# Attention: the eight PSUM banks dealt anew, four for scores and two for maximum products in place of three and three

## The chip, the cores and the metric

The kernel runs on one core of one Trainium2 chip. The metric is the device time of one execution in microseconds (us). A core has a matrix engine (TensorE, PE in the profile; its weight loads are shown apart as PEld), VectorE (DVE), ScalarE (ACT), GpSimd (POOL) and the engine that issues most of the DMAs (SyncE, SP). Matmul results go to PSUM, which has eight banks of 512 fp32 values in each of 128 partitions. Each engine works through its own instructions in order, and semaphores tie the engines together.

## The reference

One transformer layer on 2 x 2048 tokens of width 512, in fp32: attention with low-rank keys and values, and then a mixture of experts. Only the core of the attention bears on this case:

```python
scores = jnp.einsum('bhqd,bhkd->bhqk', q, k) / jnp.sqrt(jnp.float32(DH))     # b=2, h=16, q=k=2048, DH=32
scores = jnp.where(causal[None, None], scores, -jnp.inf)
attn = jax.nn.softmax(scores, axis=-1)
out = jnp.einsum('bhqk,bhkd->bhqd', attn, v)
```

The softmax subtracts the maximum of each row of scores. So the kernel needs that maximum before it takes the exponentials.

## The kernel before, in words

The program has four stages one after the other: the projections, the attention (`phase_attention`), the output projection with the shared expert, and the routed experts. The change is in the second one alone.

**Units and steps.** The 16 heads are taken four at a time and the two batches apart, which makes 8 groups. The 2048 queries of a group are cut into four chunks of 512. A unit is one group and one chunk q, so there are 32 units. A unit goes through its key tiles of 128 keys in the order that `ORDER[q]` lists (4, 8, 12 or 16 tiles). For each tile there are two steps, one for heads 0 and 1 and one for heads 2 and 3. That gives 640 steps. The four tiles of a unit that lie on the diagonal are masked: 128 of the 320 tiles, 256 of the 640 steps.

**What a step does.** TensorE computes two score products, one for each head: `b_st`, L1008, 128 keys by up to 512 queries. In a masked step VectorE then adds the mask to both banks (`b_st<-b_st,b_sooner`). ScalarE takes the exponential of each bank and writes it to one half of a buffer `b_pt` in SBUF (L928). Later TensorE uses the exponentials of both steps of a tile. The four value products (`values`, `b_ob`, L1021, 8 rows in the trace) come in the second step of the next tile. For a part of the tiles there are also four products with a matrix of ones (`count_ones`, `b_sb`, L1035), which sum the exponentials. For the other tiles (`POOL_TILES`) GpSimd adds the exponentials up in `b_acc` (L749), and one group of matmuls at the unit's end (`finish`, L1043) sums that. The values, ones and finish groups are called heavy groups below.

**The maximum products.** Between these, the same matrix engine computes the scores of a later unit a first time, transposed, only to get their row maxima: `b_mx`, L985, 128 queries by up to 512 keys. VectorE reduces each such bank to one column (L868, or on the diagonal L865, which adds the mask as it reduces). There are 1280 of them. Once a unit's maxima are complete, its row of negative maxima is made by four transposes into a `b_mx` bank (L992), ScalarE copies it (L934), and a DMA puts it under the queries as one more row. All 1312 of these (maxima and turns) form one list, `stream`. `attention_plan` decides how many of them each step takes, and `item_shares` puts a step's share in three places: after the first score product, after the heavy group, and after the second score product.

**What sets the order.** Every engine's instructions are written out by the loops in the order of the steps. The banks tie them together. A score product with the running number 2n+j goes to bank (2n+j) % NST and waits until the exponential NST before it is done (L1001). Item i of the list goes to bank i % NMX and waits until VectorE has reduced item i-NMX (or until ScalarE has copied it, where that was a turn). The values of a tile wait for the tile's last exponential, which is the one four before the second score product of their step (`values`). The scores hold NST banks, the maximum products NMX, `b_ob` and `b_sb` one each: eight in all.

**The mask.** The two banks of a masked step are one instruction (L890) where they lie next to each other, and two instructions (L894) where one is the last and one the first bank of the ring (`mask`).

Of the kernel before, what the change touches and what calls it, by code (L numbers as in the profile page):

```python
# [601 lines left out]
def phase_attention(nc, x, w, scratch, ahead, keep, heads):  # L602
# [7 lines left out]
    units, steps, first_step = attention_steps()  # L610
    stream, start, upto, turn_at, turn_step = attention_plan(units, steps, first_step)
    NS, NU = len(steps), len(units)
    NPB, NST, NMX = 8, 3, 3
    KR = HG * DH - DH
    MROW = KR

# [1378 lines left out]
def program(nc, ins, out):  # L1995
# [15 lines left out]
    with ExitStack() as ctx:  # L2011
        al = Alloc(nc, ctx)
        ahead = Ahead(al)
        keep = {
            "ident": al.sb("ident", [P, P]),
            "expert": al.sb("expert", [P, NB], I32),
            "place": al.sb("place", [P, NB], I32),
            "entry": al.sb("entry", [P, NB, TPB, 3], U32),
            "x": [tile[:].rearrange("p k n -> p (k n)").rearrange("p (t n) -> p t n", t=TPB) for tile in (ahead.oin, ahead.rin)],
            "x_in": [al.sem(f"e_rows_in{n}") for n in range(2)],  # L2020
            "entries_in": [al.sem(f"e_first_entries_in{n}") for n in range(2)],
            "weights_in": [al.sem(f"e_weights_in{n}") for n in range(2)],
        }
        with ExitStack() as early:
            heads = Heads(Alloc(nc, early))
            phase_project(nc, x, w, scratch, ahead, keep, heads)
            phase_attention(nc, x, w, scratch, ahead, keep, heads)
        begun = First(al, ahead)
        phase_shared(nc, x, w, scratch, ahead, keep, begun)
        phase_experts(nc, keep, w, scratch, begun, out)  # L2030
# [23 lines left out]
```

## Time and profile before

| | |
|---|---|
| time, median of 3 runs | 2332.29 us (2331.23 to 2332.98) |
| the profiled execution | 2336.36 us, of which the span shown is 2334.6 us |
| attention stage in the span | from about 233 to about 1440 us |
| PE busy over the span | 2192.8 us (94%) |
| DVE, ACT, POOL busy | 1480.2, 1027.3, 1165.0 us (63, 44, 50%) |

The profile gives busy and idle times of each engine. The end of a matmul is modelled: one product of 512 columns is shown with 0.40 us, while the next one can start 0.23 us behind it. So a stop of TensorE is longer than the idle time shown for it, by up to 0.17 us. The idle time shown before a weight load (PEld) is mostly time in which TensorE was still at work on a heavy group.

### The profile page before, as it was taken

To read this page: it belongs to the slowest core of one execution; us is meant where nothing else is said; L and a number is where in the kernel's file an instruction comes from. 1 tells how busy PE (TensorE), PEld (TensorE's weight loads), DVE (VectorE), ACT (ScalarE), POOL (GpSimd) and SP (SyncE) were. 2 spreads that over 40 slices of the span, in tenths; PEclk is the share of its full clock that TensorE was granted. 3 is DMA by queue.
4 is the path that set the end of the run, shared out by engine and by line. 5 is a ranking of instruction groups with operands and counts; after the bars stand their busy time and mean duration, and the time that the engine had idled before them with its cause. 6 is when DMAs were issued, how large, how long until landed. Compare 5 with 4: busy or idle time off the path is not lost. (4 is left out here: it accounts for less than half of the span.)

```text
span 2334.6 us, 32228 instructions
## 1 busy us (share of the span) xinstructions
PE 2192.8 (94%) x11695; PEld 1377.6 (59%) x11695; DVE 1480.2 (63%) x3296; ACT 1027.3 (44%) x1925; POOL 1165.0 (50%) x730
## 2 busy tenths in 40 slices
PE   6999999999999999999999997899997999999999
PEld 5777544444444444444444432677775788888887
DVE  4665886767766676676776742667565455556554
ACT  3333255555655555555555555131222343434433
POOL 1010166556665565655666557364644445544544
PEclk9999699999999999999999988899998999999999
DMA  5678702313123141151412111434433756666662
GB/s 167 246 256 268 171 24 51 77 37 91 37 55 74 38 91 37 46 142 38 91 37 55 53 30 44 127 121 134 137 105 119 240 184 222 197 215 208 207 212 87
DMA packets 168254, 278.66 MB, mean 119 GB/s; under 512 B 28571, under 2 KB 71067, under 8 KB 168096
## 3 DMA queue, kind: packets, MB, share of 16 engines
q1 hardware_dynamic: 145152, 210.43, 31.0%
q0 software_dynamic: 22944, 66.19, 9.1%
q8 instruction: 92, 1.51, 0.3%
q14 instruction: 66, 0.54, 0.1%
HBM read 191.25 MB, written 88.71 MB: 120 GB/s over the span
## 5 line engine op out<-in xcount | busy, mean ns | idle before, releaser
L928 ACT ACTIVATE b_pt<-b_st 128x512 f32<-128x512 f32 (+3 forms) x1280 | 612.5, 535 | 478.6 <-DVE b_st L890 192.0
L749 POOL TENSOR_TENSOR b_acc<-b_acc,b_pt 128x1024 f32<-128x1024 f32 (+1 forms) x256 | 593.0, 2346 | 215.8 <-ACT b_pt L928 215.2
L868 DVE TENSOR_REDUCE b_mpart<-b_mx 128x1 f32<-128x512 f32 x768 | 512.2, 686 | 186.9 <-PE b_mx L985 184.5
L1008 PE MATMUL b_st<-b_q,b_k 97*128 97x512 f32 (+2 forms) x1280 | 499.1, 403 | 57.1 <-ACT b_pt L928 53.7
L985 PE MATMUL b_mx<-b_k,b_q 96*128 96x512 f32 (+2 forms) x1280 | 510.9, 414 | 6.7 <-DVE b_mpart L868 3.3
L985 PEld LDWEIGHTS b_mx<-b_k,b_q 96*128 96x128 f32 x1280 | 249.5, 196 | 264.3 <-DVE b_mpart L868 149.7
L1008 PEld LDWEIGHTS b_st<-b_q,b_k 97*128 97x128 f32 x1280 | 243.4, 192 | 264.9 <-ACT b_pt L928 239.7
L1021 PE MATMUL b_ob<-b_pt,b_v 128*32 128x512 f32 (+3 forms) x2560 | 305.5, 549 | 1.1 <-ACT b_pt L928 1.1
L865 DVE CUSTOM_DVE_ANT_0 b_unread<-b_mx,b_later 128x384 bf16<-128x384 f32 (+3 forms) x512 | 244.6, 484 | 91.0 <-PE b_mx L985 90.5
L749 POOL TENSOR_TENSOR b_acc<-b_pt 128x1024 f32<-128x1024 f32 x48 | 113.4, 2379 | 269.5 <-ACT b_pt L928 269.5
L1774 POOL DMA_INDIRECT e_rows<-out_dram,entry x78 | 92.8, 1190 | 128.9 <-DMA out_dram<-e_rows,entry 111.9
L1902 ACT ACTIVATE e_sg<-e_fb 128x512 f32<-128x512 f32 (+3 forms) x69 | 36.6, 530 | 253.3 <-PE e_fb L79 253.3
L1866 POOL DMA_INDIRECT out_dram<-e_rows,entry x78 | 78.2, 1002 | 107.2 <-DVE e_rows L1947 90.8
L1933 DVE TENSOR_TENSOR e_hf<-e_sg,e_fb 128x512 f32<-128x512 f32 (+3 forms) x69 | 41.6, 603 | 131.3 <-ACT e_sg L1902 131.3
L1035 PE MATMUL b_sb<-b_pt,b_ones 128*32 128x512 f32 (+3 forms) x1152 | 116.5, 477 | 0.0
L890 DVE TENSOR_TENSOR b_st<-b_st,b_sooner 128x256 f32<-128x256 f32 x171 | 73.1, 428 | 67.5 <-PE b_st L1008 67.3
L77 PE MATMUL e_fb<-e_xh,e_w_split 128*128 128x512 f32 (+3 forms) x288 | 104.4, 362 | 1.8 <-PEq L1269 1.8
L1021 PEld LDWEIGHTS b_ob<-b_pt,b_v 128*32 128x32 f32 x2560 | 50.7, 108 | 90.4 <-issue 47.0
L79 PE MATMUL e_fb<-e_xl,e_w_split 128*128 128x512 f32 (+3 forms) x288 | 103.3, 359 | 0.0
L78 PE MATMUL e_fb<-e_xh,e_w_split 128*128 128x512 f32 (+3 forms) x288 | 103.0, 358 | 0.0
L77 PE MATMUL e_fb<-e_xh,e_w_guh 128*128 128x512 f32 (+3 forms) x264 | 96.9, 367 | 0.0
L79 PE MATMUL e_fb<-e_xl,e_w_guh 128*128 128x512 f32 (+3 forms) x264 | 95.9, 363 | 0.0
(251 smaller groups left out, 3692.9 us busy)
## 6 DMA issues: line engine op xcount, KB each, us to landing
b_q<-scr_qh SPq DMA_DIRECT2D x64, 256.0 KB, 4.6
b_k<-scr_kh SPq DMA_DIRECT2D x64, 256.0 KB, 4.0
sw_raw<-in_L_ffn_w_gate_dram SPq DMA_DIRECT2D x12, 704.0 KB, 4.5
sw_raw<-in_L_ffn_w_up_dram SPq DMA_DIRECT2D x12, 704.0 KB, 6.9
a_xin<-in_L_attn_x_dram POOLq DMA_DIRECT2D x8, 1024.0 KB, 5.8
scr_qh<-wo SPq DMA_DIRECT2D x8, 1024.0 KB, 5.0
scr_ql<-oin SPq DMA_DIRECT2D x8, 1024.0 KB, 7.2
scr_kh<-sw_raw SPq DMA_DIRECT2D x8, 1024.0 KB, 4.3
```

The costliest lines, as they stand in the source:

```text
L77: nc.tensor.matmul(out, wh, xh, start=first, stop=False)
L78: nc.tensor.matmul(out, wl, xh, start=False, stop=False)
L79: return nc.tensor.matmul(out, wh, xl, start=False, stop=last)
L749: g.tensor_tensor(out[:, :, lo:], so_far[:, :, lo:], pt[n % NPB][:, :, lo:], ALU.add).then_inc(s_add, 1)
L865: v.tensor_tensor_reduce(unread[i % NMX][:, 0:w], mxb[i % NMX][:, 0:w], later[:, CH - w:], 1.0, -3e38, ALU.add, ALU.max, part).then_inc(s_ ...
L868: v.tensor_reduce(part, mxb[i % NMX][:, 0:w], AX.X, ALU.max).then_inc(s_red, 1)
L928: act.activation(pt[n % NPB][:, j, lo:], stb[:, (2 * n + j) % NST, lo:], ACT.Exp, scale=SCALE).then_inc(s_exp, 1)
L985: ins = pe.matmul(bank[:, 0:max(w, 2 * P)], qb[0:KR, h, q * CH + t * P:q * CH + (t + 1) * P], kb[0:KR, h, at:at + max(w, 2 * P)], start=Tr ...
L1008: pe.matmul(stb[:, (2 * n + j) % NST, lo:], kb[:, h, at:at + P], qb[:, h, q * CH + lo:(q + 1) * CH], start=True, stop=True).then_inc(s_st, 1)
L1021: ins = pe.matmul(ob[h * DH:(h + 1) * DH, lo:], vbuf[:, kt, h * DH:(h + 1) * DH], pt[(2 * m + h // 2) % NPB][:, h % 2, lo:], start=(kt == ...
L1035: ins = pe.matmul(sb[h * DH:(h + 1) * DH, lo:], ones[:], pt[(2 * m + h // 2) % NPB][:, h % 2, lo:], start=(kt == begin), stop=(kt == ORDER ...
L1774: g.indirect_dma_start(out=tile[:, t, :], in_=rows, out_offset=None, in_offset=at).then_inc(sem, 16)
```

## The change

Two numbers. The scores get four banks and the maximum products two:

```diff
-    NPB, NST, NMX = 8, 3, 3
+    NPB, NST, NMX = 8, 4, 2
```

The order of TensorE's instructions stays the same, and so do those of ScalarE, GpSimd and SyncE. What changes is the bank that each product goes to, and with it the instruction that it waits for. A score product now waits for the exponential four before it, and an item for the reduction two before it. The plan of the items does not look at either number.

TensorE, before, in a tile that GpSimd sums (step 275 and the two behind it; `b_mx` are maximum products, `b_st` scores; the heavy group of values stands just ahead and just behind):

```order
L985 MATMUL b_mx1<-b_k,b_q 128x512 [waits b_partial_max]
L1008 MATMUL b_st<-b_q,b_k 128x512 [waits b_exp_made]
L985 MATMUL b_mx2<-b_k,b_q 128x512 [waits b_partial_max]
L1008 MATMUL b_st<-b_q,b_k 128x384 [waits b_exp_made]
L985 MATMUL b_mx0<-b_k,b_q 128x512 [waits b_partial_max]
L1008 MATMUL b_st<-b_q,b_k 128x384 [waits b_exp_made]
L985 MATMUL b_mx1<-b_k,b_q 128x512 [waits b_partial_max]
L1008 MATMUL b_st<-b_q,b_k 128x384 [waits b_exp_made]
```

TensorE, changed, at the same place:

```order
L985 MATMUL b_mx1<-b_k,b_q 128x512 [waits b_partial_max]
L1008 MATMUL b_st<-b_q,b_k 128x512 [waits b_exp_made]
L985 MATMUL b_mx0<-b_k,b_q 128x512 [waits b_partial_max]
L1008 MATMUL b_st<-b_q,b_k 128x384 [waits b_exp_made]
L985 MATMUL b_mx1<-b_k,b_q 128x512 [waits b_partial_max]
L1008 MATMUL b_st<-b_q,b_k 128x384 [waits b_exp_made]
L985 MATMUL b_mx0<-b_k,b_q 128x512 [waits b_partial_max]
L1008 MATMUL b_st<-b_q,b_k 128x384 [waits b_exp_made]
```

The sequence is the same. The third maximum product now goes to the bank of the first and the fourth to that of the second. Before, only the fourth met a bank of this group again.

VectorE, before, in steps 276 and 277 (both masked; `b_mpart` are the maxima, `b_unread` is the output of L865 that nobody reads):

```order
L890 TENSOR_TENSOR b_st<-b_st,b_sooner 128x2x128 [waits b_scores_made]
L865 ISA b_unread1,b_mpart1<-b_mx1,b_later 128x512 [waits b_item_made]
L865 ISA b_mpart1 128x1
L868 TENSOR_REDUCE b_mpart1<-b_mx2 128x1 [waits b_item_made]
L894 TENSOR_TENSOR b_st<-b_st,b_sooner 128x128 [waits b_scores_made]
L894 TENSOR_TENSOR b_st<-b_st,b_sooner 128x128
```

VectorE, changed, at the same place:

```order
L890 TENSOR_TENSOR b_st<-b_st,b_sooner 128x2x128 [waits b_scores_made]
L865 ISA b_unread0,b_mpart1<-b_mx0,b_later 128x512 [waits b_item_made]
L865 ISA b_mpart1 128x1
L868 TENSOR_REDUCE b_mpart1<-b_mx1 128x1 [waits b_item_made]
L890 TENSOR_TENSOR b_st<-b_st,b_sooner 128x2x128 [waits b_scores_made]
```

With four banks the two banks of a step always lie next to each other, so the pairs of L894 become single instructions of L890 (85 steps). Nothing else moves on VectorE.

## Rows read from the trace of the kernel before

**Rows 1.** Busy time by stretch, attention stage: us, PE, PEld, DVE, ACT, POOL, clock, DMA, GB/s
```profile
233.00:1440.00 1207.00, 1137.36 (x6607) 527.86 (x6605) 826.03 (x2176) 659.18 (x1379) 714.20 (x310) 0.97 0.26 62
```
**Rows 2.** Costliest groups of the page: busy, mean ns, idle before, releaser
```profile
L868 DVE TENSOR_REDUCE b_mpart<-b_mx 128x1 f32<-128x512 f32 x768 | 512.2, 686 | 186.9 <-PE b_mx L985 184.5
L1008 PE MATMUL b_st<-b_q,b_k 97*128 97x512 f32 (+2 forms) x1280 | 499.1, 403 | 57.1 <-ACT b_pt L928 53.7
L985 PE MATMUL b_mx<-b_k,b_q 96*128 96x512 f32 (+2 forms) x1280 | 510.9, 414 | 6.7 <-DVE b_mpart L868 3.3
L890 DVE TENSOR_TENSOR b_st<-b_st,b_sooner 128x256 f32<-128x256 f32 x171 | 73.1, 428 | 67.5 <-PE b_st L1008 67.3
```
**Rows 3.** The tile b_st, who waited for it (us, times)
```profile
  PEld b_st L1008: 241.3, 375
  PE b_st L1008: 53.7, 107
```
**Rows 4.** Timeline 780.6 to 783 us: start, duration, instruction
```profile
780.62 0.50 PE L985 MATMUL b_mx<-b_k,b_q 96*128 96x512 f32 x1
781.15 1.89 DVE L868 TENSOR_REDUCE b_mpart<-b_mx 128x1 f32<-128x512 f32 x3 [0.58 <-PE b_mx L985]
781.19 0.40 PE L985 MATMUL b_mx<-b_k,b_q 96*128 96x512 f32 x1
781.60 0.40 PE L985 MATMUL b_mx<-b_k,b_q 96*128 96x512 f32 x1
782.01 0.40 PE L985 MATMUL b_mx<-b_k,b_q 96*128 96x512 f32 x1
782.51 1.06 PE L1021 MATMUL b_ob<-b_pt,b_v 128*32 128x512 f32 x8
```
**Rows 5.** Timeline 783 to 786.8 us, the masked step behind it
```profile
783.49 0.87 ACT L928 ACTIVATE b_pt<-b_st 128x384 f32<-128x384 f32 x2 [1.51 <-DVE b_st L890]
783.51 0.50 PE L985 MATMUL b_mx<-b_k,b_q 96*128 96x512 f32 x1
784.04 0.44 PE L1008 MATMUL b_st<-b_q,b_k 97*128 97x384 f32 x1
784.05 0.69 DVE L868 TENSOR_REDUCE b_mpart<-b_mx 128x1 f32<-128x512 f32 x1
784.32 0.40 PE L985 MATMUL b_mx<-b_k,b_q 96*128 96x512 f32 x1
784.55 0.40 PE L1008 MATMUL b_st<-b_q,b_k 97*128 97x512 f32 x1
784.65 0.49 DVE L894 TENSOR_TENSOR b_st<-b_st,b_sooner 128x128 f32<-128x128 f32 x2
785.26 1.85 ACT L928 ACTIVATE b_pt<-b_st 128x384 f32<-128x384 f32 x4 [0.89 <-DVE b_st L894]
785.80 0.50 PE L1008 MATMUL b_st<-b_q,b_k 97*128 97x512 f32 x1 [0.85 <-ACT b_pt L928]
786.38 0.40 PE L1008 MATMUL b_st<-b_q,b_k 97*128 97x512 f32 x1
786.71 0.53 PE L1021 MATMUL b_ob<-b_pt,b_v 128*32 128x384 f32 x4
```
**Rows 6.** Timeline 742 to 745.6 us, a group with six items
```profile
742.97 0.75 PE L985 MATMUL b_mx<-b_k,b_q 96*128 96x256 f32 x2
743.48 0.68 DVE L868 TENSOR_REDUCE b_mpart<-b_mx 128x1 f32<-128x512 f32 x1
744.33 0.50 PE L1008 MATMUL b_st<-b_q,b_k 97*128 97x512 f32 x1 [0.61 <-ACT b_pt L928]
745.48 0.64 PE L1021 MATMUL b_ob<-b_pt,b_v 128*32 128x512 f32 x4
```
**Rows 7.** Busy time by stretch, two neighbours (columns as in Rows 1)
```profile
700.00:719.00 19.00, 18.03 (x112) 8.51 (x108) 14.49 (x39) 10.28 (x24) 14.09 (x6) 1.00 0.36 76
719.00:726.00 7.00, 6.86 (x23) 2.28 (x23) 2.40 (x6) 2.53 (x6) 0.00 (x0) 0.52 1.10 236
```

## The prediction, written before the changed kernel had run

> **What bounds the kernel now.** I read the busy table first, then the stretches, the costliest groups, the waits by tile and last the timeline of a few steps. The change touches the attention stage alone. There TensorE is busy 1137 of 1207 us [rows 1]. VectorE with 826 us, ScalarE with 659 and GpSimd with 714 are well below. So TensorE sets the pace, and only its stops can give or take time: whatever the others gain or lose counts when TensorE waits for it. Its stops are shown before the scores, 53.7 us in 107 waits, all for an exponential [rows 2, 3]. Before the maximum products it stops for 3.3 us only [rows 2]. The reader is to see here that the bank kind that gets one more is the one that waits, and the kind that gives one up does not wait today. The question is how far below "one bank too few" the maximum products are.
>
> **Units of time.** In [rows 4, 5], at full clock, a product of 512 columns follows another at 0.23 us (784.32 to 784.55). The first product behind a heavy group costs 0.34 (780.62 to 781.19 is 0.57 for two). The first result of a group reaches VectorE after 0.53 (780.62 to 781.15). A reduction takes 0.69, but a second one starts 0.60 behind it: three in 1.89 are 2 x 0.60 + 0.69. The exponential of ScalarE that begins at 785.26 has 384 columns. The pair before it took 0.87 for two, so one takes 0.48 and ends at 785.74. TensorE goes on at 785.80, so a release costs 0.06.
>
> **Part A, one bank fewer for the maximum products.** A heavy group takes TensorE 1.0 us (782.51 to 783.51), long enough for VectorE to catch up. So what counts is how many items stand between two heavy groups. I counted that in the order of TensorE's instructions: none to two items in 298 gaps, three in 64, four in 55, five in 33, six in 27, and seven or eight in 8 (one more, at the stage's start, is left out). With alternating scores the items of a gap start at 0, 0.57, 1.03, 1.50, 1.96 and 2.43 us. With two banks item k waits for reduction k-2, that is until 0.53 + 0.60 (k-3) + 0.69 + 0.06: 1.28 for the third, 1.88, 2.48 and 3.08 for the fourth to sixth. With three banks these times hold one item later, so today the fifth goes at 1.96 and the sixth at 2.48. The loss per gap is 0.25, 0.38, 0.52, 0.60 and 0.60 us. The sum is 64 x 0.25 + 55 x 0.38 + 33 x 0.52 + 27 x 0.60 + 8 x 0.60 = 16 + 21 + 17 + 16 + 5 = 75 us.
>
> A gap of the trace bears this out. In [rows 4] the four items start at 780.62, 781.19, 781.60 and 782.01. Reductions one and two end at 781.84 and 782.44. With two banks the third goes at 781.90 and the fourth at 782.50, which is 0.49 late, and the values behind it start 0.49 late. Nothing hides that: the values are on TensorE itself.
>
> Some of it is hidden, though. In gaps of six TensorE stands for an exponential anyway. In [rows 6] the second of the two items at 742.97 goes at about 743.3, and with two banks it would wait for the reduction that ends at 744.16, so until 744.22. But the score behind it stands until 744.33 today. The loss at the group's end is about 0.1 in place of 0.60. I take 0.45 off for each of the 27 gaps of six: -12. **Part A is +63 us.** Its bounds are 0 (TensorE stops only 3.3 us for these banks now, and if the wait fell wholly into other waits nothing would be seen) and 93 (each reduction at 0.69 without the overlap, which makes the losses 0.29, 0.51 and 0.69).
>
> **Part B, one bank more for the scores.** The stops to be had are the idle time of 53.7 us. To it comes for each of the 107 the tail of the modelled end, 0.40 - 0.23 = 0.17, so 18 us. The 375 - 107 = 268 waits that only the weight load shows [rows 3] lie inside that tail, at about 0.09 each, so 24 us. Together that is 96 us. Not all of it comes back. The masked step in [rows 5] shows why. Its stops are 784.04 (0.19 late, since 783.51 + 0.34 is 783.85) and 785.80 (784.55 + 0.23 is 784.78, so 1.02 late). With four banks the first goes at 783.85. The next item goes at 784.1 and the score after it at 784.4. The one that stood until 785.80 now waits for an exponential that ended at 784.36 (783.49 + 0.87), so it goes at 784.6. But the score behind that needs the exponential that ends at 785.74. That one hangs on the mask at 784.65, which VectorE takes only once its reduction (784.05) is done. So it goes at 785.80, the values start at about 786.2 in place of 786.71, and 0.51 of 1.21 us is gained, 42%. The wait moves on by two products. I take 42% of 96: **part B is -40 us.** Bounds: 0 (the chain score, mask, exponential, values holds everything) and -96.
>
> **Small edits.** In 85 steps two mask instructions become one. [Rows 5] show the two with 0.49, and the single one takes 0.43 [rows 2]. That is 0.06 times 85 = 5 us on VectorE, of which a part is on the path: -0 to -5, I take -1. The turns lose their third bank too. An item two behind a turn then waits for ScalarE's copy, but a heavy group or a few products stand between, so I put 0 for 32 of them, and at most 32 x 0.3 = 10.
>
> **Sum.** +63 - 40 - 1 + 0 = +22 us. The profiled execution took 2336.4, so it would be 2358.5. The median of the runs lies 4.1 lower, so I forecast 2355.
>
> **A rule that speaks against the change.** In 719 to 726 us the granted clock is 0.52, so mostly the lower of its two levels (1.2 GHz), where it was 1.00 in the 19 us before [rows 7]. Ahead of it TensorE had stood a few times before scores. The Trainium skill says in "TensorE: Matmul & The Clock Gate", section "A second HAM failure mode: psum-queue depth-cycling", that a kernel that cycles through PSUM banks idles so often and so briefly between matmul groups that the clock gate swings between its levels. By that rule part A's many small stops would bring more such stretches, and part B's would take some away. The attention shows a mean clock of 0.97 [rows 1], which is 0.03 x 2 x 1207, about 70 us, at half speed at most, and costs 36 us at most. The rule has its own case below.
>
> **The rivals.**
> - **The fourth score bank is worth more** (16%). Masks and exponentials follow earlier scores, so the gain in one gap may help the next. For it: all of TensorE's shown waits stand before scores [rows 2]. Against: the wait in [rows 5] hangs on the mask. With 96 us back and +63 it is -33, so about 2300. It wins from the point where part B returns more than two thirds of its stops. The Trainium skill ("Perfetto Trace Analysis", section "Optimization Strategy") says that the same gap repeated on the engine that should be saturated can mean too little PSUM. By it alone the kind with the visible gap is the one to widen. The trace agrees on the gap, but not on who pays for it.
> - **It cancels out** (10%). The two examples show it, +0.49 in one gap and -0.51 in the next. If the gaps were equally many, about 2332. Against: the counts (187 gaps with three or more items, 128 masked tiles).
> - **The fourth bank gives nothing** (12%). The values wait for the exponential four before the second score of their step, which is just what that score waits for with four banks. If the values stand in its place, B is -5 and the sum +57: 2390.
> - **The clock** (10%). With more short stops the half-speed time grows by a half: 18 us more, 2373. The other way, it falls by as much, and 2337 results.
>
> The likeliest case, +22 with 2340 to 2370, gets 52%. A measurement of this kernel tells about 0.2%, 5 us, from no change. Faster than that: the first rival and half of the second, 0.20. Same: 0.07. Slower: 0.73. The range that holds 8 in 10 runs from 2314 to 2392, from half-way into the first rival to the third.
>
> **What would show it.** Right: the idle time before L1008 falls from 57 to under 30 us and the one before L985 rises from 7 to 35 or more, released by L868. The timeline has items that stand for a reduction in gaps of three and more, above all in tiles that GpSimd sums. L894 is gone. The stages outside 233 to 1440 us keep their times, and VectorE's busy time falls by about 5 us. Wrong: idle time before L985 that stays under 15 us, or idle time that moves to the values (L1021).

## The result, and the profile after

The changed kernel takes 2367.92 us (median; 2366.97 to 2370.01), and the one before 2332.64. The ratio is 1.0154 (95% interval 1.0136 to 1.0171), so the change costs 35 us. The profiled executions give 2366.97 and 2336.36 us, a difference of 30.6, and the spans differ by the same 30.6. The prediction said 2355, in a range of 2314 to 2392.

All of it lies in the attention. By stretch the changed kernel shows (us, then PE, PEld, DVE, ACT and POOL busy, granted clock, DMA share, GB/s):

```profile
233.00:1471.00 1238.00, 1170.17 (x6607) 520.76 (x6605) 831.20 (x2091) 658.35 (x1377) 714.26 (x310) 0.97 0.24 60
1471.00:2365.20 894.20, 846.66 (x4103) 680.56 (x4095) 522.25 (x883) 290.96 (x425) 427.77 (x388) 0.97 0.53 167
```

The same TensorE instructions (6607) now take 1238 us where [rows 1] have 1207. What follows takes 894.2 us, against 2334.6 - 1440 = 894.6 before. The costliest groups of the page have changed places:

```profile
L868 DVE TENSOR_REDUCE b_mpart<-b_mx 128x1 f32<-128x512 f32 x768 | 516.2, 687 | 220.7 <-PE b_mx L985 216.5
L985 PE MATMUL b_mx<-b_k,b_q 96*128 96x512 f32 (+2 forms) x1280 | 550.4, 436 | 48.4 <-DVE b_mpart L868 29.5
L1008 PE MATMUL b_st<-b_q,b_k 97*128 97x512 f32 (+2 forms) x1280 | 480.5, 392 | 10.4 <-ACT b_pt L928 9.3
L890 DVE TENSOR_TENSOR b_st<-b_st,b_sooner 128x256 f32<-128x256 f32 x256 | 109.2, 426 | 75.9 <-PE b_st L1008 75.9
```

The idle time before the scores fell from 57.1 to 10.4 us, and the one before the maximum products rose from 6.7 to 48.4 [rows 2]. Idle time alone gives only -5 for the two. The rest is shown as busy time, which rose by 33 us over the stage (1137 to 1170). A product of 512 columns that follows a stop, or a heavy group, is shown with 0.50 us in place of 0.40, and the mean of L985 rose from 414 to 436 ns.

The place of [rows 4] shows it in the changed kernel (timeline: start, duration, instruction):

```profile
806.01 0.50 PE L985 MATMUL b_mx<-b_k,b_q 96*128 96x512 f32 x1
806.55 1.98 DVE L868 TENSOR_REDUCE b_mpart<-b_mx 128x1 f32<-128x512 f32 x3 [0.73 <-PE b_mx L985]
806.58 0.40 PE L985 MATMUL b_mx<-b_k,b_q 96*128 96x512 f32 x1
807.29 0.50 PE L985 MATMUL b_mx<-b_k,b_q 96*128 96x512 f32 x1
807.63 0.34 PE L1008 MATMUL b_st<-b_q,b_k 97*128 97x384 f32 x1
807.89 0.50 PE L985 MATMUL b_mx<-b_k,b_q 96*128 96x512 f32 x1
808.49 1.07 PE L1021 MATMUL b_ob<-b_pt,b_v 128*32 128x512 f32 x8
```

The first reduction ends at 806.55 + 0.69 = 807.24, and the third product goes 0.05 later. The third comes 0.71 behind the second and the fourth 0.60 behind the third, which are the steps worked out in the prediction (781.19 to 781.90 to 782.50). From the first item to the values it is 2.48 us, against 1.89 in [rows 4]: 0.59 late, where 0.49 was forecast. In this gap the missing 0.10 is the restart. Behind a stop the next product comes at 0.34 (807.29 to 807.63) and not at 0.23.

The masked steps behind it answer to [rows 5]:

```profile
809.49 0.50 PE L985 MATMUL b_mx<-b_k,b_q 96*128 96x512 f32 x1
809.83 0.34 PE L1008 MATMUL b_st<-b_q,b_k 97*128 97x384 f32 x1
810.01 0.40 PE L985 MATMUL b_mx<-b_k,b_q 96*128 96x512 f32 x1
810.24 0.62 PE L1008 MATMUL b_st<-b_q,b_k 97*128 97x512 f32 x2
811.17 1.36 ACT L928 ACTIVATE b_pt<-b_st 128x384 f32<-128x384 f32 x3 [1.32 <-DVE b_st L890]
811.72 0.50 PE L1008 MATMUL b_st<-b_q,b_k 97*128 97x512 f32 x1 [0.44 <-ACT b_pt L928]
812.14 0.53 PE L1021 MATMUL b_ob<-b_pt,b_v 128*32 128x384 f32 x4
```

The reader is to see the wait moved on by two products. The two scores at 810.24 go together, where the second stood until 785.80 before. The next one stands until 811.72. From 809.49 to the values it is 2.65 us, against 3.20: 0.55 gained, with 0.51 forecast.

### The profile page after: what moved, and what is told of

It reads as the page before. It is cut to its first block and busy times, and to the rows that moved or that the text cites. A ratio compares the mean times of both kernels' runs of the same rounds, so it can differ in the third digit from the quotient of the medians.

```text
span 2365.2 us, 32143 instructions
## 1 busy us (share of the span) xinstructions
PE 2223.3 (94%) x11695; PEld 1369.4 (58%) x11695; DVE 1485.6 (63%) x3211; ACT 1027.5 (43%) x1925; POOL 1163.2 (49%) x730
## 5 line engine op out<-in xcount | busy, mean ns | idle before, releaser
L868 DVE TENSOR_REDUCE b_mpart<-b_mx 128x1 f32<-128x512 f32 x768 | 516.2, 687 | 220.7 <-PE b_mx L985 216.5
L985 PE MATMUL b_mx<-b_k,b_q 96*128 96x512 f32 (+2 forms) x1280 | 550.4, 436 | 48.4 <-DVE b_mpart L868 29.5
L1008 PE MATMUL b_st<-b_q,b_k 97*128 97x512 f32 (+2 forms) x1280 | 480.5, 392 | 10.4 <-ACT b_pt L928 9.3
L985 PEld LDWEIGHTS b_mx<-b_k,b_q 96*128 96x128 f32 x1280 | 247.5, 194 | 398.2 <-DVE b_mpart L868 247.6
L1008 PEld LDWEIGHTS b_st<-b_q,b_k 97*128 97x128 f32 x1280 | 242.7, 192 | 168.7 <-ACT b_pt L928 111.5
L865 DVE CUSTOM_DVE_ANT_0 b_unread<-b_mx,b_later 128x384 bf16<-128x384 f32 (+3 forms) x512 | 245.6, 484 | 101.1 <-PE b_mx L985 100.2
L890 DVE TENSOR_TENSOR b_st<-b_st,b_sooner 128x256 f32<-128x256 f32 x256 | 109.2, 426 | 75.9 <-PE b_st L1008 75.9
```

Source lines behind the costliest of these rows:

```text
L865: v.tensor_tensor_reduce(unread[i % NMX][:, 0:w], mxb[i % NMX][:, 0:w], later[:, CH - w:], 1.0, -3e38, ALU.add, ALU.max, part).then_inc(s_ ...
L868: v.tensor_reduce(part, mxb[i % NMX][:, 0:w], AX.X, ALU.max).then_inc(s_red, 1)
L890: v.tensor_tensor(block, block, sooner[:].unsqueeze(1).to_broadcast([P, 2, P]), ALU.add).then_inc(s_msk, 1)
L985: ins = pe.matmul(bank[:, 0:max(w, 2 * P)], qb[0:KR, h, q * CH + t * P:q * CH + (t + 1) * P], kb[0:KR, h, at:at + max(w, 2 * P)], start=Tr ...
L1008: pe.matmul(stb[:, (2 * n + j) % NST, lo:], kb[:, h, at:at + P], qb[:, h, q * CH + lo:(q + 1) * CH], start=True, stop=True).then_inc(s_st, 1)
```

## The experiments

Each run was timed beside the kernel before on the same chip. The times are medians. A ratio is against before, with its 95% interval. "Lost to the clock" is (1 - mean granted clock) x span, so what the stretches at the lower level cost at most: 63 us before (0.973), 61 us in the changed kernel (0.974).

**Seven banks, part A alone.**

```diff
-    NPB, NST, NMX = 8, 3, 3
+    NPB, NST, NMX = 8, 3, 2
```

> Seven banks: three for scores, two for maximum products, so part A alone. Theory 1 (the two parts are separate: A is the wait for a reduction in gaps of three and more items, B the stops before scores behind masked steps): the changed kernel's trace shows about 74 us more stops before items and 63 us fewer before scores, so this one should be 60 to 95 us over before, 2393 to 2428. Rival (the fourth score bank gave nothing and the whole +35 us is part A): 2368, as with four and two.

Measured: 2419.13 us, ratio 1.039 (1.0356 to 1.0423). Its costliest groups:

```profile
L985 PE MATMUL b_mx<-b_k,b_q 96*128 96x512 f32 (+2 forms) x1280 | 547.8, 434 | 45.9 <-DVE b_mpart L868 28.9
L1008 PE MATMUL b_st<-b_q,b_k 97*128 97x512 f32 (+2 forms) x1280 | 495.5, 400 | 44.6 <-ACT b_pt L928 42.2
```

and its span and mean granted clock:

```profile
core 0: 2416.6 us, clock 0.968
```

The third maximum bank was worth 82 us of span (2416.6 - 2334.6) and the fourth score bank 51 (2416.6 - 2365.2). The items' row is that of the changed kernel. The scores' row has 44.6 us of idle time against 57.1, so the new stops swallow about a fifth of the old ones. The two parts are separate in the main, and the rival in which the fourth bank gives nothing is refuted. (Part B has no run of its own: three maximum banks and four score banks would need a ninth bank.)

The 82 us rest on one traced execution of each kernel. The medians taken side by side differ by 91.5 us (2419.13 - 2327.62). Part of that is the clock: the seven executions of the kernel before in that comparison have 0.976 to 0.981, the traced one has 0.973.

Part of A and of B is the clock. Here up to 0.032 x 2416.6 = 77 us are lost to it, 14 more than before and 16 more than in the changed kernel. At an equal clock part A is about 68 us and part B about 36. These are estimates: the clock has three digits, which is 1 us in each term, and time at the lower level costs nothing where TensorE stands anyway.

The two traces also show where part A lies. The same 486 gaps between heavy groups follow each other in both. The table takes each from the last product of one heavy group to the last product of the next, and sorts them by the items in them. In the last column half of the time at the lower clock level is taken out.

| items in the gap | gaps | loss forecast for each, us | longer with seven banks, all together, us | for each, at an equal clock, us |
|---|---|---|---|---|
| 0 to 2 | 298 | 0 | 1.1 | -0.01 |
| 3 | 64 | 0.25 | 17.3 | 0.18 |
| 4 | 55 | 0.38 | 13.2 | 0.30 |
| 5 | 33 | 0.52 | 17.1 | 0.53 |
| 6 | 27 | 0.60, less 0.45 | 18.3 | 0.62 |
| 7 or 8 | 8 | 0.60 | 4.3 | 0.36 |
| ahead of the first heavy group | 1 | left out | 10.2 | 5.4 |

So the loss stands where the forecast put it, in gaps of three and more items, and it grows with their number up to six.

**No masks.** The mask on VectorE is left out, the exponentials wait for the scores alone, and their scale is 20 times smaller so that all values stay finite.

```diff
-                    if steps[n][2] >= TPC * steps[n][1]:
-                        mask(n)
...
-                        if kt >= TPC * q:
-                            act.wait_ge(s_msk, masked(n) + 1)
-                        else:
-                            act.wait_ge(s_st, 2 * n + j + 1)
+                        act.wait_ge(s_st, 2 * n + j + 1)
```

> Three and three banks, the mask of the scores left out on VectorE (256 steps), the exponentials wait for the scores alone; their scale is made 20 times smaller so that all values stay finite. Theory 1: the stops before scores stand behind masks, 65 to 80 us go, 2250 to 2270. Rival (ScalarE's pace makes them): only VectorE's 5 to 15 us go, 2315 to 2330.

> The same without the mask, with four and two banks. Theory 1: without masks the fourth score bank has nothing to give and the loss of the third maximum bank stands alone: 60 to 90 us over the one with three and three. Rival (what four score banks give has nothing to do with masks): again about 35 us over it.

Measured: 2256.47 us with three and three (ratio 0.9705, 0.9679 to 0.9732) and 2342.99 with four and two (1.0071, 1.0044 to 1.0099). Without masks TensorE hardly stops before the scores (its row, three and three banks):

```profile
L1003 PE MATMUL b_st<-b_q,b_k 97*128 97x512 f32 (+2 forms) x1280 | 483.0, 394 | 11.0 <-ACT b_pt L923 9.8
```

So most of the stops come from the mask in the chain of score, mask and exponential, and ScalarE's own pace leaves 10 us of idle time. The same deal of the banks now costs 86.5 us in place of 35. What the fourth score bank gave is gone with the masks, and part A stands alone, as in the run with seven banks (82 us of span, 91.5 in the medians). Leaving the mask out also takes its work off VectorE, so this run does not tell the chain from VectorE's load. The next but one does in part, since there VectorE does the same work in another order.

**Short reductions.** Each reduction reads 128 columns at most. The maxima are then not the true ones, and the scale is 20 times smaller.

```diff
+                    m = min(w, P)
...
-                        v.tensor_reduce(part, mxb[i % NMX][:, 0:w], AX.X, ALU.max).then_inc(s_red, 1)
+                        v.tensor_reduce(part, mxb[i % NMX][:, 0:m], AX.X, ALU.max).then_inc(s_red, 1)
```

> Three and three banks; every reduction reads only the first 128 columns of its bank (the maxima are then not the true ones; the exponentials' scale is made 20 times smaller so that all values stay finite). A reduction takes 0.28 us in place of up to 0.69. Theory 1: items' stops go and masks come sooner: 2270 to 2315.

> The same short reductions with four and two banks. Theory 1: with 0.53 + 0.28 + 0.06 = 0.87 us a bank is free again before the third item's natural time of 1.03, so part A is gone and only what the fourth score bank gives is left: 10 to 50 us faster than the one with three and three. Rival (the loss is a fixed cost of each wait or of turns, not the reduction's length): again 20 to 40 us slower than it.

Measured: 2279.55 us with three and three (0.9792, 0.9763 to 0.982) and 2262.65 with four and two (0.9724, 0.9696 to 0.9752). The reductions of the second (from the view of the tile `b_mx`: duration ns min/median/max):

```profile
L869 DVE TENSOR_REDUCE b_mpart<-b_mx x768: 221/291/294, 248.1 to 1304.8; 128x1 f32<-128x128 f32 x192
```

With reductions of 0.29 us the sign turns: four and two is 17 us faster. So nearly all of part A's loss is the length of the reduction and not a fixed cost of having two banks. A little is left: TensorE's idle time before the maximum products is 4.1 us with three and three and 11.2 with four and two. The short reductions also let the masks start sooner, so these runs do not size part B.

**The mask ahead of one reduction on VectorE.** In a masked step VectorE reduces the item between heavy group and second score before it masks. Here the mask goes first, where that item is a single one and no turn.

```diff
+                    first = item_shares(n)[1]
+                    if some - first > 1 or any(what[0] == "turn" for what in stream[first:some]):
+                        first = some
-                    for i in range(here, some):
+                    for i in range(here, first):
...
-                    for i in range(some, there):
+                    for i in range(first, there):
```

> Three and three banks; on VectorE the mask of a step comes ahead of the reduction of the item that stands between heavy group and second score, where that is a single one. Theory 1: the mask starts up to 0.6 us sooner in part of the 256 masked steps, so of the 79 us of stops before scores 15 to 40 go: 2295 to 2320. Rival (the reductions are what is short, and a later one holds the items): no change or up to 15 us slower.

> Four and two banks, with the mask ahead of the single reduction between heavy group and second score. Theory 1: stops before scores are down to 16 us, so an earlier mask gives little, while the reduction that comes later now holds an item two on: 0 to 25 us slower than four and two, 2368 to 2393. Rival (masks still set the pace): 10 to 25 us faster, 2343 to 2358.

> Three and three banks with the mask ahead of the single reduction on VectorE, on the same chip as the two above: again 30 to 36 us under before, 2292 to 2300.

Measured: with three and three banks 2294.46 us (0.9868, 0.9841 to 0.9895), and again 2295.22 (0.9854, 0.9835 to 0.9873). With four and two 2393.28 (1.0294, 1.0253 to 1.0334). The order that gains 33 us with three and three loses 25 with four and two (30 when each is taken against the kernel before beside it). The first and the last of these lie at the very edge of what was expected, half a us below 2295 and 0.3 above 2393. With four and two the scores hardly wait, and the reduction that comes later holds an item (L988 is the product line of this kernel, four and two banks):

```profile
L988 PE MATMUL b_mx<-b_k,b_q 96*128 96x512 f32 (+2 forms) x1280 | 555.1, 439 | 64.1 <-DVE b_mpart L868 45.9
```

TensorE's idle time before these products is 64.1 us, where the changed kernel has 48.4.

**The other deal.**

```diff
-    NPB, NST, NMX = 8, 3, 3
+    NPB, NST, NMX = 8, 2, 4
```

> The deal the other way: two banks for scores, four for maximum products. Theory 1: items wait for reductions in 75 places for 14 us today, so a fourth bank can give 14 us at most; each score then waits for the exponential two before it, so masked steps stand for the whole chain of product, mask and exponential: 256 steps at 1 us or more, less the 79 us of today: 2480 to 2700. Rival (score banks are not short, only reductions are): 2320 to 2350.

Measured: 2905.16 us, ratio 1.2474 (1.2408 to 1.2539), far outside both expectations. The costliest row, the attention stage by stretch, and the clock:

```profile
L1008 PE MATMUL b_st<-b_q,b_k 97*128 97x512 f32 (+2 forms) x1280 | 629.2, 498 | 286.6 <-ACT b_pt L928 282.2
```

```profile
233.00:2000.00 1767.00, 1474.94 (x6592) 630.66 (x6591) 840.48 (x2091) 689.65 (x1378) 713.75 (x310) 0.78 0.17 42
```

```profile
core 0: 2898.0 us, clock 0.856
```

TensorE is busy 1475 of 1767 us there, and its mean clock is 0.78. Up to 0.144 x 2898 = 417 us are lost to the clock, 354 more than before. The rest, at least 210 us of the 563, is the waits. Taken so, that part is the mechanism that was expected (2905 - 354 = 2551 lies in its range), but 354 is the most that the clock can have cost, since at the lower level TensorE also stood. What was missed is what such waits do to the clock.

**Items behind the second score.** In masked steps the items between heavy group and second score move behind that score, on TensorE and on VectorE. In a second version those ahead of the heavy group move too.

```diff
-        return [here + (there - here) * k // 3 for k in range(4)]
+        marks = [here + (there - here) * k // 3 for k in range(4)]
+        if steps[n][2] >= TPC * steps[n][1]:
+            marks[2] = marks[1]
+        return marks
```

> Three and three banks; in the masked steps the items that stood between the heavy group and the second score product come behind that product, on TensorE and so on VectorE too. Theory 1: the second score comes about 0.25 us sooner and its mask has one reduction less ahead of it, in all masked steps and not only where a single item stood there. So it gains at least what the earlier mask gave (33 us) and up to the 71 us that no mask at all gave: 2265 to 2295. Rival (the bunched items now wait for their reductions): 2300 to 2330.

> The same, and the items ahead of the heavy group go behind the second score too. Theory 1: the items ahead of the heavy group cost the mask nothing where that group stands between, and three or more items in a row wait for reductions: 0 to 15 us slower than the one above.

Measured: 2293.33 us (0.9845, 0.9828 to 0.9862) and 2298.36 (0.9862, 0.9842 to 0.9882). The first is at the slow end of what was expected and not to be told from the earlier mask alone. The order of the instructions shows why: a single item stands between heavy group and second score in 134 of the 256 masked steps, five items in 2 and none in 120, so the two edits act on nearly the same steps.

**A mask for each head.** On top of the items behind the second score:

```diff
-                    v.wait_ge(s_st, 2 * n + 2)
...
+                    for j in range(2):
+                        v.wait_ge(s_st, 2 * n + j + 1)
+                        block = stb[:, (b0 + j) % NST, d * P:(d + 1) * P]
+                        v.tensor_tensor(block, block, sooner[:], ALU.add).then_inc(s_msk, 1)
...
-                            act.wait_ge(s_msk, masked(n) + 1)
+                            act.wait_ge(s_msk, 2 * masked(n) + j + 1)
```

> Three and three banks, items behind the second score in masked steps, and the mask in two instructions, one for each head, each as soon as its own score is there; the first head's exponential waits for its own mask alone. Theory 1: the first exponential no longer hangs on the second score product, so the first bank comes free up to 1 us sooner; VectorE pays about 0.06 to 0.15 us more in each of 256 steps: 2265 to 2290. Rival (VectorE's order is what holds now, and the extra instructions cost more than they give): 2293 to 2310.

Measured: 2274.46 us, ratio 0.9773 (0.975 to 0.9796). It beats both kernels: 53 us under before, where the items behind the second score alone gave 37. Its rows:

```profile
L1006 PE MATMUL b_st<-b_q,b_k 97*128 97x512 f32 (+2 forms) x1280 | 493.4, 403 | 21.6 <-ACT b_pt L926 20.2
L983 PE MATMUL b_mx<-b_k,b_q 96*128 96x512 f32 (+2 forms) x1280 | 482.8, 405 | 8.0 <-DVE b_mpart L871 4.1
L893 DVE TENSOR_TENSOR b_st<-b_st,b_sooner 128x128 f32<-128x128 f32 x512 | 138.9, 294 | 100.8 <-PE b_st L1006 98.4
```

VectorE pays 138.9 - 109.2 = 30 us more than with one mask instruction for each step, off the path. The stops before scores fall from 57.1 to 21.6 us with all three maximum banks kept.

## Why the prediction was right

The sign and the mechanism were right, and the size of the sum was about a third short (+22, measured +31 in the profiled executions and +35 in the medians).

- **Part A** was put at +63. Alone it costs 82 us of span, 68 at an equal clock. In the gaps of three and more items the traces give 65 us at an equal clock, so the 63 came out, but in part by luck. The 12 us taken off as hidden in gaps of six are not hidden: these gaps lost 0.62 us each (17 us together), where 0.15 (4 us) was left of the forecast. The gaps of three and four lost less than was worked out (28 us in place of 37), and the two errors cancel. Why they lost less was not tested. One difference is that every reduction was taken at 0.69 us, while those of the diagonal (L865) have a mean of 0.48 and a read-out of 0.08 behind it. The restart of 0.10 us is inside these losses. Products of 512 columns shown with 0.50 us that do not stand behind a heavy group are 111 before and 258 with seven banks (at full clock), so restarts make about 147 x 0.10 = 15 us of part A. What the sum left out is the stretch ahead of the first heavy group, 10 us, and the clock.
- **Its upper bound** of 93 has a slip. By the forecast's own steps, reductions of 0.69 without overlap lose 0.25 us in a gap of three and 0.47 in one of four, and not 0.29 and 0.51. That gives 89, and changes nothing else.
- **Part B** was put at -40. It is -51 of span, -36 at an equal clock. The run without masks shows that the stops hang on the mask, and the gap behind the mask shows that the wait moves on by two products. The 42% come from a single masked step and were applied to all waits, so that the size is this near is luck in part.
- **The clock** was priced at up to 18 us either way, as one rival. It works in both parts, +14 in A and -16 in B, and cancels in the sum (-2). The mean clock is 0.973 before, 0.968 with seven banks, 0.974 after. For A this is clear of the spread (0.967 to 0.970 in four executions, 0.976 to 0.981 in seven of the kernel before beside them). For B it compares executions that did not run side by side. The Trainium skill's rule on cycling through PSUM banks ("TensorE: Matmul & The Clock Gate", section "A second HAM failure mode: psum-queue depth-cycling") agrees with the runs in which stops were added alone (0.968) or grew large (0.856). It does not by itself decide on a change that trades one kind of stop for another.
- **The masks.** L890 and L894 were to cost 5 us less on VectorE, and they do: 73.1 + 41.8 us before, 109.2 now. The row of L894 before:

```profile
L894 DVE TENSOR_TENSOR b_st<-b_st,b_sooner 128x128 f32<-128x128 f32 x170 | 41.8, 292 | 27.2 <-PE b_st L1008 27.1
```

  Yet VectorE's busy time rose by 5.4 us over the span (1480.2 to 1485.6), so that sign to look for was wrong. In part it is the reductions (L868 from 512.2 to 516.2). Reductions that follow at once overlap, and overlapping time counts once. Three took 1.89 us in [rows 4] but 1.98 here.
- **The turns** were put at 0. The changed kernel shows idle time for ScalarE's copy before `b_mx` 23 times, 12.1 us, of which 2.3 us stand before products and the rest before weight loads. The kernel before has one such time, 0.6 us.

```profile
  ACT b_rows L934: 12.1, 23
```

  What it costs on the path was not tested by itself. The bound of 10 us is not contradicted.
- **The signs to look for:** before L1008 under 30 us was named and 10.4 came, before L985 35 or more and 48.4 came, L894 is gone, and the other stages kept their times. Only VectorE's busy time went the other way.
- **The rivals.** That it cancels out is refuted, since part A is larger than part B by more than the noise. That the fourth bank is worth much more would need 64 us or more back, and 51 came.

## What to carry to other kernels

A ring of banks has to be as deep as the burst of products that one consumer must clear at its own pace. Count the products between two long pieces of other work and compare their spacing with the consumer's: the idle time shown today (3 us here) says nothing about the next bank taken away (68 us). Before a bank is moved to the side that waits, ask what the wait hangs on. Here it hung on a mask behind a reduction, and two edits of the order and grain of the masks gave 53 us, with no bank moved.

## What the runs showed of the hardware

TensorE's clock is part of the price of small stops. With seven banks in place of eight it was 0.967 to 0.970 in four executions, against 0.976 to 0.981 of the kernel before beside them. The share of the stage in which TensorE is busy went from 94% (1137 of 1207 us) to 83% with two score banks, and the mean clock of the stage from 0.97 to 0.78, though no stop before a score there was longer than 2.0 us (the waits for an exponential, total and times and longest):

```profile
PE b_st L1008 <- ACT b_pt L928: 282.2, 342, 2.0
```

A product that follows a stop delays the next one by 0.10 us more than one in a run of products does (0.34 against 0.23 us for 512 columns). The stage of the changed kernel shows this 468 times at full clock behind products of 0.50 us (0.33 or 0.34), and 712 times 0.23 or 0.24 behind products of 0.40.
